# The first scan stage's input term made by TensorE through diagonals of B, in place of a GpSimd product with broadcast rows

## The reference, cut to what matters

```python
dt, Bm, Cm = jnp.split(x_dbl, [DT_RANK, DT_RANK + D_STATE], axis=-1)
dt = jax.nn.softplus(jnp.einsum('blr,rd->bld', dt, W_dt) + b_dt)
A = -jnp.exp(A_log)
dA = jnp.exp(jnp.einsum('bld,dn->bldn', dt, A))
dBu = jnp.einsum('bld,bln->bldn', dt * u, Bm)

def step(hc, inp):
    dA_t, dBu_t, C_t = inp
    hc = dA_t * hc + dBu_t
    y_t = jnp.einsum('bdn,bn->bd', hc, C_t)
    return (hc, y_t)
```

## Time and profile before

| What | us |
|---|---|
| median of the three runs | 5039.34 |
| the profiled execution: its span | 5046.6 |
| first scan of the stage starts (L370) | 60.62 |
| last `take_y` of the stage starts (L580) | 996.60 |
| last output addition of the stage (L587) | 1005.09 |
| PE busy between 60 and 996.6 | 761.49 of 936.6 |
| VectorE busy, same stretch | 888.11 |
| GpSimd busy, same stretch | 884.62 |
| ScalarE busy, same stretch | 561.84 |

### The profile page before, as it was taken

The page is one execution under the profiler, slowest core; times in us unless marked ns, Lnnn a source line. Parts: engine busy times, 40 slices in busy tenths (PEclk is TensorE's granted clock), DMA queues, the critical chain, the costliest instruction groups (busy, mean ns, idle before and its releaser), DMA issues.

```text
span 5046.6 us, 49393 instructions
## 1 busy us (share of the span) xinstructions
PE 3946.2 (78%) x15216; PEld 2274.4 (45%) x15218; DVE 2845.7 (56%) x4948; ACT 2217.0 (44%) x4098; POOL 2475.4 (49%) x2152
## 2 busy tenths in 40 slices
PE   6888888759947778897788769977965788887892
PEld 2333333347724445675333346645642333333671
DVE  6999999941146664211888842236334666554422
ACT  5566666321147664112555533333334444445241
POOL 5999999822212333111888944433455311112256
PEclk9999999959968888998888879987986799999896
DMA  5666665422210100321555521123347222211145
GB/s 152 158 161 151 161 160 159 127 77 85 84 56 17 34 26 9 105 102 53 150 153 145 145 82 46 44 90 94 92 131 154 72 40 39 39 27 46 46 137 131
DMA packets 312121, 476.73 MB, mean 94 GB/s; under 512 B 34890, under 2 KB 167990, under 8 KB 311786
## 3 DMA queue, kind: packets, MB, share of 16 engines
q1 hardware_dynamic: 277152, 388.87, 29.1%
q0 software_dynamic: 29184, 76.12, 5.4%
q10 hardware_dynamic: 5504, 8.39, 0.6%
HBM read 375.26 MB, written 97.49 MB: 94 GB/s over the span
## 4 chain that ended last, share of the span: by engine, by line
PE 39%; POOL 7%; DVE 6%; issue 5%; ACT 4%; DMA 3%; SPq 0%; DVEq 0%; ACTq 0%; POOLq 0%; another core or an unknown queue 0%
PE s_gate_up L2305 8%; PE s_result_sum L2321 4%; PE s_out_sum L3676 3%; PE s_hidden_sum L1745 3%; PE s_result_sum L1756 3%; PE s_scores_T L3660 3%; POOL s_h L435 2%; PE s_shared L2961 2%; DVE s_maxima L3308 2%; PE s_scores L3617 2%; POOL s_gathered L1047 1%; PE s_shared L2971 1%; POOL s_h L444 1%; PE s_transposed L2295 1%; PE s_mid_transposed L2314 1%
## 5 line engine op out<-in xcount | busy, mean ns | idle before, releaser
L435 POOL TENSOR_TENSOR s_h<-s_dtu,s_bc 128x1024 f32<-128x1024 f32 x384 | 904.0, 2363 | 78.4 <-PE s_y_sum L477 61.9
L477 PE MATMUL s_y_sum<-s_h,identity 128*128 128x512 f32 x1536 | 776.3, 643 | 158.2 <-POOL s_h L444 150.4
L402 ACT ACTIVATE s_decay<-s_dt,s_A 128x512 f32<-128x512 f32 x768 | 498.3, 681 | 330.2 <-DVE s_h L377 323.4
L477 PEld LDWEIGHTS s_y_sum<-s_h,identity 128*128 128x128 f32 x1536 | 296.5, 203 | 600.4 <-issue 305.3
L3482 ACT ACTIVATE s_weights_T<-s_scores_T 128x1024 f32<-128x1024 f32 (+3 forms) x384 | 292.2, 809 | 311.9 <-PE s_scores_T L3660 309.7
L2305 PE MATMUL s_gate_up<-s_w_gate_up,s_rowsT 128*128 x1184 | 420.5, 488 | 2.8 <-issue 2.4
L3308 DVE TENSOR_REDUCE s_maxima<-s_scores 128x1 f32<-128x512 f32 (+3 forms) x440 | 282.6, 659 | 218.7 <-PE s_scores L3621 140.0
L444 POOL TENSOR_TENSOR s_h<-s_h,s_bc 128x512 f32<-128x512 f32 x288 | 367.1, 1275 | 23.6 <-DVE s_h L370 14.9
L3530 POOL TENSOR_SCALAR_AFFINE_SELECT s_weights_T<-s_weights_T 128x256 f32<-128x256 f32 x256 | 103.2, 408 | 541.2 <-ACT s_weights_T L3482 538.6
L2364 DVE TENSOR_TENSOR s_mid<-s_act,s_gate_up 128x128 f32<-128x128 f32 (+1 forms) x228 | 92.9, 407 | 454.7 <-ACT s_act L2337 430.2
L370 DVE TENSOR_TENSOR_SCAN s_decay<-s_decay,s_carry,s_h 128x512 f32<-128x512 f32 x240 | 303.1, 1276 | 24.5 <-POOL s_clip_flag L2633 13.8
(11 more groups left out here) (533 smaller groups left out, 7739.6 us busy)
## 6 DMA issues: line engine op xcount, KB each, us to landing
s_bc<-s_bc_rows SPq DMA_DIRECT2D x384, 512.0 KB
sorted_results<-s_result SPq DMA_DIRECT2D x160, 128.0 KB
s_w_inter<-in_L_ffn_experts_inter SPq DMA_DIRECT2D x16, 1024.0 KB
s_w_exp_out<-in_L_ffn_experts_out SPq DMA_DIRECT2D x16, 1024.0 KB
s_queries<-parts_of_q SPq DMA_DIRECT2D x96, 128.0 KB
s_keys<-parts_of_k SPq DMA_DIRECT2D x96, 128.0 KB
results_by_token<-zeros SPq DMA_DIRECT2D x16, 512.0 KB, 6.1
s_pair<-results_by_token SPq DMA_DIRECT2D x16, 512.0 KB
```

The lines of the kernel that those rows point to most:

```text
L402: S.e.activation(self.decay[:, (2 * g + d) % 4, :], dt[q // self.passes % 2][:, at, :], ACT.Exp, scale=A[:, at, g % ns:g % ns + 1]).then_i ...
L435: G.e.tensor_tensor(self.h[r][:], dtu[q // self.passes % 2][:, at:at + 2, :], mid(self.bc[r][:, 0, :], 2), ALU.mult).then_inc(*self.fed.up())
L477: made = T.e.matmul(self.y[:, d, :], ident[:], self.h[r][:, d, :], start=False, stop=g % ns == ns - 1)
```

## The change

`mamba_stage` uses a new class `FedScan`; the later stage keeps `Scan`. dt*u, 128x1024 for a pass, still comes from GpSimd, but into `soft`. TensorE turns it by time (`turn_dtu`, 8 transposes for each pass), and ScalarE copies it to `by_time`. TensorE also turns B (4 small matmuls for a chunk) into `b_columns`. From these ScalarE makes, for each state and each 128 steps, a diagonal matrix of B, 64 for a chunk. A half's input term is then 4 matmuls, each with 128x128 of `by_time` stationary and a diagonal of 128 columns moving, into the PSUM ring `feed`. The decays go to the SBUF ring `h` and are made 3 units ahead. VectorE scans them with the term in PSUM and multiplies nothing by C; GpSimd multiplies both halves in one instruction. Only the rows of C are broadcast. The ticks of the side work are set anew, and the prologue has 60 ticks in place of 58. Of its parameters, `shares=(0,)` means VectorE weighs nothing and `own_diagonals=4` means ScalarE makes every diagonal. The diff, cut to its core:

```diff
+class FedScan:
+    RING, LEAD, SOON = 6, 3, 6
...
+        self.h = [M.sb(f"h{i}", [P, 2, CH]) for i in range(self.RING)]
+        self.c_rows = [M.sb(f"c_rows{i}", [P, CH]) for i in range(self.RING)]
+        self.carry = M.sb("carry", [P, self.per, 2])
+        self.b_columns = [M.sb(f"b_columns{i}", [P, TPC, ns]) for i in range(2)]
+        self.diagonal = M.sb("b_diagonals", [P, ns, TPC, P])
+        self.feed = M.ps("feed", [P, 4, CH])
+        self.y = M.ps("y_sum", [P, 2, CH])
...
+    def program(self, begin, unit, end, early=nothing, front=nothing, late=nothing, back=nothing, spread=None):
...
+        soon = lambda c: spread(c, range(self.SOON), 2 * self.per - 2 * self.SOON)
+        later = lambda c: spread(c, range(self.SOON, self.ns), 0)
...
+        first.until(whole)
+        Side(soon(0)).until(whole)
+        begin()
...
+    def vector(self, take_y, **sides):
...
+            for d in range(2):
+                V.wait_ge(*self.decayed.at(2 * g + d))
+                V.wait_ge(*self.fed.at(2 * g + d))
+                h, feed = self.h[r][:, d, :], self.feed[:, (2 * g + d) % 4, :]
+                V.e.tensor_tensor_scan(
+                    feed if d < k else h, h, feed,
+                    self.carry[:, i, d:d + 1] if c % CPB else 0.0, ALU.mult, ALU.add).then_inc(*self.scanned.up())
+                if d == 0:
+                    beside(2 * i)
...
+    def scalar(self, dt, A, dt_made, **sides):
...
+        def decays(g):
+            if g < self.units:
+                q, r = g // ns, g % self.RING
+                S.wait_ge(*dt_made.at(q))
+                S.wait_ge(*self.summed.at(g - self.RING))
+                for d in range(2):
+                    at = q % self.passes * 2 + d
+                    S.e.activation(self.h[r][:, d, :], dt[q // self.passes % 2][:, at, :], ACT.Exp,
+                                   scale=A[:, at, g % ns:g % ns + 1]).then_inc(*self.decayed.up())
+
...
+        def unit(c, i, g, beside):
+            k = self.share(g)
+            decays(g + self.LEAD)
+            beside(2 * i)
+            beside(2 * i + 1)
+            if self.has_next(g):
+                S.wait_ge(*self.scanned.at(2 * g + 1))
...
+                if self.by_scalar(n):
+                    S.wait_ge(*self.columns_made.at(c))
+                    S.wait_ge(*self.fed_last(c - 1, n))
+                    for t in range(TPC):
+                        made = S.e.activation(self.diagonal[:, n, t, :], self.K.ident[:], ACT.Copy,
+                                              scale=self.b_columns[c % 2][:, t, n:n + 1])
+                    made.then_inc(*self.diagonal_s.up())
+
+    def gpsimd(self, **sides):
...
+        def weigh(g):
+            k, r = self.share(g), g % self.RING
+            if k < 2:
+                h = self.h[r][:, k:2, :]
+                G.wait_ge(*self.scanned.at(2 * g + 1))
+                G.wait_ge(*self.c_here[r].at(g // self.RING))
+                if self.has_next(g):
+                    G.wait_ge(*self.carried_at(g))
+                G.e.tensor_tensor(h, h, mid(self.c_rows[r][:], 2 - k), ALU.mult).then_inc(*self.weighed_g.up())
+
+    def tensor(self, skip, u, u_made, by_time, by_time_made, **sides):
+        T, ns, ident = self.K.T, self.ns, self.K.ident
+
+        def feed(g, d):
+            if g >= self.units:
+                return
+            c, n, q = g // self.per, g % ns, g // ns
+            at = q % self.passes * 2 + d
+            T.wait_ge(*by_time_made.at(q))
+            T.wait_ge(*self.diagonal_at(c, n))
+            T.wait_ge(*self.scanned.at(2 * (g - 2) + d if g >= 2 else -1))
+            if g >= 2 and d < self.share(g - 2):
+                T.wait_ge(*self.vector_weighed(g - 2))
+                if self.has_next(g - 2):
+                    T.wait_ge(*self.carried_v_at(g - 2))
+            for t in range(TPC):
+                made = T.e.matmul(self.feed[:, (2 * g + d) % 4, t * P:(t + 1) * P], by_time[c % 2][:, t, at * P:(at + 1) * P],
+                                  self.diagonal[:, n, t, :], start=True, stop=True)
+            made.then_inc(*self.fed.up())
+
+        def total(g, d):
+            if g < 0:
+                return
+            q, r, k = g // ns, g % self.RING, self.share(g)
+            at = q % self.passes * 2
+            if g % ns == 0 and d == 0:
+                T.wait_ge(*self.y_taken.at(q - 1))
+                T.wait_ge(*u_made.at(q // self.passes))
+                for e in range(2):
+                    T.e.matmul(self.y[:, e, :], skip[:, at + e, :], u[q // self.passes % 2][:, at + e, :], start=True, stop=False)
+            T.wait_ge(*(self.vector_weighed(g) if d < k else self.gpsimd_weighed(g)))
+            made = T.e.matmul(self.y[:, d, :], ident[:], self.h[r][:, d, :], start=False, stop=g % ns == ns - 1)
+            if d == 1:
+                made.then_inc(*self.summed.up())
+
+        def begin():
+            for d in range(2):
+                feed(0, d)
+
+        def unit(c, i, g, beside):
+            for d in range(2):
+                feed(g + 1, d)
+                total(g - 2, d)
+                beside(2 * i + d)
+
...
 def mamba_stage(K, W):
-    sc = Scan(K, M, PASSES, NS, (1, 1, 1, 2), prologue=58)
+    sc = FedScan(K, M, PASSES, NS, (0,), prologue=60, own_diagonals=4)
...
+            yield 47
+            S.wait_ge(*columns_sum.at(c))
+            S.wait_ge(*sc.diagonal_at(c - 2, NS - 1) if c > 1 else sc.diagonal_g.at(-1))
+            S.e.activation(sc.b_columns[c % 2][:], bank[:, 1, 0:TPC * 2 * NS].rearrange("p (t n) -> p t n", t=TPC)[:, :, 0:NS],
+                           ACT.Copy).then_inc(*sc.columns_made.up())
+            yield 49
             log_term(2 * c)
+            yield 58
+            turned_dtu(2 * c)
+
+        def turned_dtu(q):
+            pair = slice(q % 2 * 2 * P, (q % 2 * 2 + 2) * P)
+            S.wait_ge(*dtu_turned.at(q))
+            S.wait_ge(*sc.fed.at(2 * (q - 3) * NS - 1 if q > 3 else -1))
+            S.e.activation(by_time[q // 2 % 2][:, :, pair],
+                           bank[:].rearrange("p a (t e) -> p (a t) e", t=2), ACT.Copy).then_inc(*by_time_made.up())
 
         def log_term(q):
             S.wait_ge(*dtp_made.at(q))
-            S.wait_ge(*dt_made.at(q - 1))
+            S.wait_ge(*dtu_turned.at(q - 1))
...
-            G.wait_ge(*sc.fed.at((q - 3) * NS - 1))
-            G.e.tensor_tensor(dtu[r][:, pair, :], dt[r][:, pair, :], u[r][:, pair, :], ALU.mult).then_inc(*dtu_made.up())
+            G.e.tensor_tensor(soft[:], dt[r][:, pair, :], u[r][:, pair, :], ALU.mult).then_inc(*dtu_made.up())
...
+            yield 46
+            T.wait_ge(*rows_made.at(c))
+            for t in range(TPC):
+                made = T.e.matmul(bank[:, 1, t * 2 * NS:(t + 1) * 2 * NS], rows[32:64, t * P:(t + 1) * P], K.ident[32:64, 32:64],
+                                  start=True, stop=True)
+            made.then_inc(*columns_sum.up())
+            free[1] = sc.columns_made.at(c)
+            yield 48
             delta(2 * c)
+            yield 57
+            turn_dtu(2 * c)
+
+        def turn_dtu(q):
+            T.wait_ge(*dtu_made.at(q))
+            both_free()
+            for t in range(TPC):
+                for d in range(2):
+                    made = T.e.transpose(bank[:, t // 2, t % 2 * 2 * P + d * P:t % 2 * 2 * P + (d + 1) * P],
+                                         soft[:, d, t * P:(t + 1) * P], K.ident[:])
+            made.then_inc(*dtu_turned.up())
+            free[:] = [by_time_made.at(q)] * 2
 
```

More of the change, by code:

```diff
@@ L517, in mamba_stage @@
     late_t = M.sb("conv_late_term", [P, ND, 3])
-    zs, u, dt, dtu = ([M.sb(f"{n}{i}", [P, ND, CH]) for i in range(2)] for n in ("z", "u", "dt", "dtu"))
+    zs, u, dt = ([M.sb(f"{n}{i}", [P, ND, CH]) for i in range(2)] for n in ("z", "u", "dt"))
+    by_time = [M.sb(f"dtu_by_time{i}", [P, TPC, DI]) for i in range(2)]
     bank = M.ps("front", [P, 2, CH])
@@ L536, in sync @@
         zeros = K.sync_zero_rows()
-        sc.sync(rows_made, rows[32:64, :], lambda g: steps(zeros, 1 if g % 8 == 7 else 0))
+        sc.sync(rows_made, rows[48:64, :], lambda g: steps(zeros, 1 if g % 8 == 7 else 0))
         steps(zeros, 1000)
@@ L541, in early @@
         def early(c):
-            yield 34
+            yield 13
             V.wait_ge(*K.x_here[c].at(0))
-            yield from ln.vector_stats(c, X[:, chunk_tiles(c), :], 34)
+            yield from ln.vector_stats(c, X[:, chunk_tiles(c), :], 13)
         def front(c):
-            for d, tick in enumerate((23, 26, 30, 33)):
+            for d, tick in enumerate((22, 24, 28, 30)):
                 taken = bank[:, d % 2, :]
@@ L571, in late @@
         def late(c):
-            yield 7
+            yield 6
             delta(2 * c + 1)
@@ L624, in front @@
                     *h_made.up())
-            for d, tick in enumerate((20, 21, 28, 31)):
+            for d, tick in enumerate((20, 21, 26, 28)):
                 yield tick
@@ L662, in late @@
         def late(c):
```

(27 more changed lines are left out.)

156 lines of the change are left out of this document (138 added, 18 removed).

## The result

The changed kernel takes 5299.15 us (median of 4 runs, 5292.07 to 5303.37), against 5041.32 us for the kernel before beside it: a ratio of 1.0509, with a 95% interval of 1.0496 to 1.0523. The change costs 258 us. The profiled execution has a span of 5290.3 us, 243.7 more than that of before; up to the end of the stage it is 252.9 more, and the rest of the program, which the change does not touch, came out 9 us shorter in it.

What follows compares the result with a forecast made beforehand. VectorE and GpSimd together bound the kernel before; PE, with 270 us of room, would become the only bound. Loop +254 and prologue +10 give 264 us more, 5303 on the median 5039.3; range 5240 to 5400.

Steps and rivals of the forecast that it cites:

- The bound: Loop: PE's need becomes 1161 us, exceeding its room by 225 us, so PE becomes the only bound.
- The rival that keeps PE's idle time on top of its work (5450): Loop: PE's present 175 us idle stays on top of its 1161 us need, +400; chance 0.12.
- The feed, 471 us: PE in the loop: 512 halves at 0.92 us each, 471 us, with bounds 451 and 558.
- rival (2): PE's feed: a stream of new operands runs denser, 0.083 us a record, feed 340 us, total 5170; chance 0.04.
- Rival (3): PE's feed: one pass for each diagonal product; loop 918, or 835 without latency (time 4948); chance 0.03 faster, 0.01 tie.
- Rival (4): ScalarE: its diagonals hold up the feed, a few us a chunk, inside the range; no separate chance given.
- Density, 98%: PE in the loop: busy 98% of the time, taken from a PE-bound stretch of the next stage; need 1161 becomes 1185.
- The wait for `take_y`, 5 us: PE, first total of each pass: waits for `take_y` some 0.3 us, 16 times, 5 us.
- The tail: End of the stage, last `take_y` to the output addition: 8.5 us, as in the kernel before.
- The loop, 1190: Loop of the stage: 1190 us, for 936 in the kernel before, so 254 more.
- The prologue, 10 us: Before the first scan: transposes, copy, 24 diagonals and first decay with table load add 10 us, 5 to 13.
- The other engines: Loop: GpSimd falls to 643 us, VectorE to 680, ScalarE rises to 735, all under PE.

Runs made afterwards that it cites:

- the two runs that take work from it: Changed kernel without half 1's identity matmuls except each pass's last state: 1.0141 of before; changed kernel with dt*u by time and diagonals in bf16: 1.0016.
- The dose runs: Kernel before with the identity matmul adding half 0 to the y sum issued twice (the first dose): 1.0053; with both halves' issued twice: 1.0417.
- the narrow run: Changed kernel with 64 columns of each diagonal moving in place of 128, from the third unit on: 1.0518 of the kernel before.
- the bf16 run: Changed kernel with dt*u by time and the diagonals kept in bf16, one record for each feed matmul: 1.0016 of the kernel before.
- the weighing on VectorE: Changed kernel with products by C divided between VectorE and GpSimd as in the kernel before, shares 1, 1, 1, 2: 1.0565 of the kernel before.
- the split feed: Kernel before with some of 16 states fed by TensorE: 4 states 1.0384, reordered with 6 row buffers 1.0088, then 3 states 1.0090, or bf16 1.0044.
- b_half_0_twice: Kernel before with the identity matmul that adds half 0 of each unit to the y sum issued twice: 1.0053 of the kernel before.
- h_six: Kernel before with 4 of 16 states fed by TensorE, 6 row buffers, both halves of a fed unit made before the sums: 1.0088 of before.

## Why the prediction was right

**The time.** Forecast 5303 and measured 5299.15; 264 us more was forecast, 258 measured. By stages of the profiles, the last output addition moved from 1005.09 to 1257.99, 252.9 us.

**The bound.** That PE would become the only bound is shown by its 98.5% at clock 1.00 and by the two runs that take work from it, which returned 186 of 205 us and 250 of 312. The rival that keeps PE's idle time on top of its work (5450) is out: it wanted 175 us idle, and the loop has 17. The dose runs on the kernel before say the same from the other side.

**The feed, 471 us** at 0.92 a half. Measured 0.89, 456 us. It was 15 too high, most of the 20 us that were put on top of the lower bound of 451. The first weight load that lies open in L3602's group hides in a stream, as argued. But there was luck in the working. Eight records have 7 steps and not 8, so the division should have given (1.16 - 0.285) / 7 = 0.125 us a record. In the trace the first of these steps is 0.213 and the other six are 0.112 each: dividing by 8 came out right because the first step is nearly two. By 0.125 the feed would have been 512 us and the forecast some 5345, inside the range, but 46 us off.

The Trainium skill, page "TensorE: Matmul & The Clock Gate", has 81 ns a record in "Back-to-back issue gap". Here 0.112 us was measured over 4096 records in f32, so rival (2) is out for this type; in bf16 the spacing was less than the page's, 0.055. What that page of the Trainium skill gives in "LDWEIGHTS" is columns / 1.2, and so 107 ns. In f32 the narrow run agrees, as 64 columns moving still left 0.112 us between most records; in bf16 the loads followed each other at 0.055, so as a spacing it does not hold there, and the measurement decides.

**Faster.** Rival (3) needed one record for each matmul. The trace has 4096 for 2048 matmuls of L722. And its price was too good: the bf16 run has exactly that single record, at 0.055 us, and came out at a loop of 926.6 where the rival said 835. What it left out is that the short records no longer hide the load of the f32 sums, and that with the engines closer together less of the saved work returns.

**ScalarE's diagonals.** Rival (4) priced them at a few us a chunk. The feed waited 2.4 us for them in the whole stage, and the run with GpSimd making them had the same loop.

**Density, 98%.** With the measured feed the need is 667 + 456 + 23 = 1146, 97.4% of 1176.5. Where PE's need lies nearer to its neighbours' it is worse: 96.7% with both sums twice (1105 of 1143), 95% without half 1's sums (941 of 990), 92% with one sum twice (886 of 959), 90% with the feed in bf16 (1146 less 312, 834 of 927). The number was taken from a stage with idle neighbours; by these four runs it held because the change made this loop one too.

**The wait for `take_y`, 5 us.** Measured 6.4. **The tail**, 8.5: measured 1257.99 - 1249.50 = 8.49.

**The loop, 1190.** Measured 1176.5; with the measured feed the same sum gives 1146 / 0.98 + 5 = 1174, so the 15 us too many in the feed explain the difference.

**The prologue, 10 us.** Measured 72.99 - 60.62 = 12.4. Six runs with this same prologue have their first scan between 70.6 and 73.3, and three with that of before between 59.7 and 60.6, so 10 to 13 is what can be said. The path that the prediction added up is steadier: from the end of dt*u to the first scan it is 12.1 us in each of the six and 2.5 in each of the three, 9.7 more where 10.3 had been added up. What varies lies ahead of it: dt*u is done between 58.4 and 61.1 in the six, and between 57.2 and 58.2 in the three. Whether B's turning, for which nothing was added, has a part in that is not settled. The 24 diagonals took 7.10 for 7.6. That they need not stand on this path was not seen; GpSimd takes some 7 us of it away.

**The other engines.** GpSimd 658 for 643 forecast, ScalarE 704 for 735, VectorE 737 for 680. VectorE's is the worst: 208 us of products were subtracted whole, but the union of busy time fell only by 151, since records of VectorE that follow each other overlap and the sum of durations counts that twice: over the loop that sum exceeds the union by 82 us in the kernel before and by 22 in the changed one. It decided nothing here. The scans did stay at 1.22 and 1.28, and a decay into SBUF takes 0.714 in place of 0.681, 17 us on an engine with 470 to spare.

**Where the experiments went against my reading.** Three times an expectation from needs alone was too good: the first dose on the kernel before, the weighing on VectorE, and the split feed. In each of them more wait stood in front of an engine that was at or near its bound: GpSimd's `feed` for the y sums in the first and the third (42.8 and 68.9 us for 20.3), PE's feed in the second (33.0 for 3.6).

## What to carry to other kernels

Before work is moved to an engine with room, its room has to be read from record spacings, not from its busy share, and set against the whole of what is moved: here 270 us of room stood against 494, and no relief of the two engines that bounded could make up for it. A product with a diagonal was no cheaper here than any matmul of its shape: built of 128x128 f32 blocks it paid 0.11 us a record for the weight load and for the columns side by side, and halving one of them alone gained next to nothing.

With three engines busy for 84 to 96% of this loop (b_half_0_twice, h_six), the sum of needs was too optimistic, by 23 us of 936 and by 38 at least. There the ring that the newly busy engine fills deserves a look: what frees the buffer, and what is queued behind that wait.
